# Two graph layers on one core: the destination index read in 2 KB rows and turned on TensorE, and the first three groups of scatters sent to two tables

## The reference

```
layer 1   neigh[src[e]] += edge_weight[e] * x[dst[e]]          for every edge e
          x1 = layernorm(x + branch(x, W_self) + branch(neigh, W_neigh))
          branch(v, W) = standardise(relu(v @ W.T + b)) * scale + offset
layer 2   f = linear(x1); weight = silu(edge_attr_64 @ W_fc1) @ W_fc2
          m[dst[e]] += products of weight, f[src[e]] and edge_attr_4[e]
          out = layernorm(x1 + cos(angle) * sc(x1) + sin(angle) * lin(m))
```

## Time and profile before

| what | value |
|---|---|
| time, median of 3 runs | 5498.28 us (5498.08 to 5500.08) |
| the profiled execution's own time | 5497.89 us |
| its span, first to last instruction | 5496.1 us |
| mean granted TensorE clock | 0.716 of full speed |
| setup, to SP's first load of the node pass | 112.8 us |
| node pass, to the last scatter | about 2956 us |
| all that follows | about 2427 us |

### The profile page before, as it was taken

One profiled execution on the slowest core, in us unless ns is written; L12 is line 12 of the kernel. 1 busy time (PEld: TensorE's weight loads), 2 busy tenths in 40 slices (PEclk: granted clock), 3 DMA queues, 4 the chain that ended last, 5 costly groups with the idle time before them and its releaser, 6 DMA issues. The chain is left out here.

```text
span 5496.1 us, 83091 instructions
## 1 busy us (share of the span) xinstructions
PE 3528.2 (64%) x18413; PEld 2923.1 (53%) x18413; DVE 2741.1 (50%) x11175; ACT 2615.7 (48%) x9201; POOL 4067.5 (74%) x3277
## 2 busy tenths in 40 slices
PE   1555555555555555555555377888888888888872
PEld 0443343344334334334434255888888888888871
DVE  2655555555565555565555384333333333333338
ACT  0322222222222222222222255888888888888863
POOL 0888888888888888888888654777777777777750
PEclk9766666666666666676677577777777777777765
DMA  8666666666666666666665683333333333333323
GB/s 225 120 117 111 111 116 114 112 112 112 111 117 115 111 111 115 116 111 112 112 113 99 130 204 105 81 81 79 81 81 79 81 81 81 79 81 81 79 74 127
DMA packets 748229, 588.07 MB, mean 107 GB/s; under 512 B 336911, under 2 KB 616360, under 8 KB 745111
## 3 DMA queue, kind: packets, MB, share of 16 engines
q0 software_dynamic: 286576, 224.93, 29.6%
q1 hardware_dynamic: 446066, 310.47, 20.9%
q10 hardware_dynamic: 15542, 52.19, 2.4%
HBM read 374.65 MB, written 212.60 MB: 107 GB/s over the span
## 5 line engine op out<-in xcount | busy, mean ns | idle before, releaser
L705 POOL DMA_INDIRECT sums_scratch<-vals,to_i x1568 | 2447.4, 1561 | 616.5 <-issue 506.4
L992 POOL DMA_INDIRECT fg<-f_scratch,src_e x1568 | 1486.4, 948 | 501.6 <-issue 477.3
L1045 ACT ACTIVATE hot<-raw,e_s 128x40 f32<-128x40 f32 x6272 | 1392.3, 313 | 346.2 <-DVE raw L1068 317.5
L619 PE MATMUL ps_n<-same,hot 128*40 128x128 f32 x3136 | 694.3, 414 | 1326.8 <-issue 1324.9
L619 PEld LDWEIGHTS ps_n<-same,hot 128*40 128x40 f32 x3136 | 556.0, 184 | 1436.2 <-issue 1371.8
L662 ACT COPY near<-ps_n 40x512 f32<-40x512 f32 x196 | 113.3, 578 | 1636.3 <-PE ps_n L619 1636.3
L1021 PE MATMUL ps_eu<-hot,prod 128*128 128x120 f32 x3136 | 889.3, 378 | 0.0
L1019 PEld LDWEIGHTS ps_eu<-hot,prod 128*128 128x128 f32 x3136 | 622.3, 244 | 305.4 <-DVE prod L1075 253.9
L1074 DVE TENSOR_TENSOR prod<-ps_ew,fg 128x256 f32<-128x256 f32 x392 | 164.6, 420 | 1239.3 <-DMA fg<-f_scratch,src_e 1239.3
L1019 PE MATMUL ps_eu<-hot,prod 128*128 128x40 f32 x3136 | 618.9, 288 | 248.0 <-DVE prod L1075 247.0
L1021 PEld LDWEIGHTS ps_eu<-hot,prod 128*128 128x128 f32 x3136 | 619.6, 245 | 0.0
(11 more groups left out here) (193 smaller groups left out, 3833.8 us busy)
## 6 DMA issues: line engine op xcount, KB each, us to landing
srow_s<-in_src SPq DMA_DIRECT2D x196, 512.0 KB, 3.5
e_s<-in_edge_attr SPq DMA_DIRECT2D x196, 256.0 KB, 3.7
hid_scratch<-hid SPq DMA_DIRECT2D x196, 256.0 KB, 3.6
hid_e<-hid_scratch SPq DMA_DIRECT2D x196, 256.0 KB
sums_scratch<-zeros ACTq DMA_DIRECT2D x24, 1056.0 KB, 26.8
sums_scratch<-vals,to_i POOLq DMA_INDIRECT x1568
fg<-f_scratch,src_e POOLq DMA_INDIRECT x1568
t_in<-sums_scratch POOLq DMA_DIRECT2D x72, 256.0 KB, 6.7
```

The source lines that it names most:

```text
L619: last = pe.matmul(ps_n[t // TH][:, t % TH, :], hot[:, k, t, :], same[:, k, t, :], start=True, stop=True)
L705: pool.indirect_dma_start(out=sums_d[i], out_offset=bass.IndirectOffsetOnAxis(ap=to_i[:, j, t:t + 1], axis=0), in_=vals[:, j, t, :], in_of ...
L992: pool.indirect_dma_start(out=fg[:, j, t, :], out_offset=None, in_=f_d, in_offset=bass.IndirectOffsetOnAxis(ap=src_s[:, j, t:t + 1], axis= ...
L1045: last = act.activation(hot[:, k, t, c, :], raw[:, k, t, :], ACT.Copy, scale=e4_s[:, j, t, c:c + 1])
```

## The change

Three things change. First, `dst` is loaded in rows of 512 edges (2 KB), one row for a half: 98 partitions by 4 rows, in three transfers. The last row of the last group is filled with FAR beforehand, so only its 320 own edges are loaded. DVE casts it to `dst_r`, takes least and greatest of each half by reducing along the row, and PE turns `dst_r` into the old layout by 16 transposes of strided columns, which DVE copies from PSUM to `dstf`. The chain that computed the extremes over partitions goes. PE does this ahead of the transposes of the weights, and DVE copies `bias4` later. Second, ACT clears the tables in the order of tables, with a semaphore for each. Third, POOL sends the scatters of the first PAIRS = 3 groups to tables 0 and 1 in turn (t % 2), waits for the clearing of tables 0 and 1 before the first scatters of group 0 and for that of tables 2 and 3 at group 3, and its count of earlier scatters to a table follows from that.

```diff
+            dst_i = tmp("dst_i", [98, 4, HE], I32)
+            dst_r = tmp("dst_r", [98, 4, HE])
+            own = tmp("own", [98, HE])
...
-                    full = a["dst"][0:NFULL * SG].rearrange("(s h p k) -> p (s h) k", h=2, p=P, k=TH)
-                    sp.dma_start(dst_i[:, 0:2 * NFULL, :], full).then_inc(dst_in, 16)
-                    sp.dma_start(dst_i[:, 2 * NFULL:NH, :],
-                                 a["dst"][LAST:E].rearrange("(h p k) -> p h k", h=2, p=P)).then_inc(dst2_in, 16)
+                    sp.dma_start(dst_i[:, 0:3, :], a["dst"][0:3 * 98 * HE].rearrange("(g r e) -> r g e", g=3, r=98)).then_inc(dst_in, 16)
+                    sp.wait_ge(far_set, 1)
+                    sp.dma_start(dst_i[0:96, 3, :], a["dst"][3 * 98 * HE:NFULL * SG].rearrange("(r e) -> r e", r=96)).then_inc(dst2_in, 16)
+                    sp.dma_start(dst_i[97:98, 3, TWICE - HE:HE],
+                                 a["dst"][NFULL * SG:E].rearrange("(o e) -> o e", o=1)).then_inc(dst2_in, 16)
...
-                    for z in range(ZSPLIT):
-                        for i in range(NTAB):
+                    for i in range(NTAB):
+                        for z in range(ZSPLIT):
                             act.dma_start(sums_d[i].rearrange("(p r) d -> p (r d)", p=P)[:, z * ZPART:(z + 1) * ZPART],
-                                          zeros[:, :]).then_inc(z_st, 16)
+                                          zeros[:, :]).then_inc(z_st[i], 16)
...
+                    dve.memset(dst_i[:, 3, :], int(FAR)).then_inc(far_set, 1)
                     dve.memset(lin_f[:, :, :], 0.0).then_inc(zeroed, 1)
-                    dve.wait_ge(dst2_in, 16)
                     dve.wait_ge(dst_in, 16)
-                    link(dve.tensor_copy(dstf[:, :, :], dst_i[:, :, :]))
...
+                    dve.tensor_copy(dst_r[:, 0:3, :], dst_i[:, 0:3, :]).then_inc(rows_f, 1)
+                    dve.wait_ge(dst2_in, 32)
+                    dve.tensor_copy(dst_r[:, 3, :], dst_i[:, 3, :]).then_inc(rows_f, 1)
+                    dve.wait_ge(rows_f, 2)
+                    dve.tensor_reduce(ext[:, 0, :], dst_r[:, :, :], AX.X, ALU.min)
+                    dve.tensor_reduce(ext[:, 1, 0:3], dst_r[:, 0:3, :], AX.X, ALU.max)
+                    link(dve.scalar_tensor_tensor(out=own[:, :], in0=dst_r[:, 3, :], scalar=FAR, in1=dst_r[:, 3, :],
+                                                  op0=ALU.is_lt, op1=ALU.mult))
+                    link(dve.tensor_reduce(ext[:, 1, 3:4], own[:, :], AX.X, ALU.max))
...
+                    dve.wait_ge(rows_t, 1)
+                    for k in range(TH):
+                        last = dve.tensor_copy(dstf[:, :, k], ps_d[k][:, :, :].rearrange("p g r -> p (g r)"))
+                    link(last)
+                    dve.tensor_copy(dst0[:, :, :], dstf[:, :, :])
...
+                    pe.wait_ge(rows_f, 2)
+                    for k in range(TH):
+                        for g in range(4):
+                            last = pe.transpose(ps_d[k][:, g, :], dst_r[:, g, k:HE:TH], ident[0:98, 0:98])
+                    last.then_inc(rows_t, 1)
...
-                        pool.wait_ge(z_st, 16 * NTAB * ZSPLIT)
+                        def adds_so_far(i, s, t):
+                            if isinstance(s, int) and s < PAIRS:
+                                return s * 2 * PER + t // 2
+                            return (PAIRS * 2 * PER if i < 2 else 0) + (s - PAIRS) * PER + t // NTAB
...
+                            pair = isinstance(s, int) and s < PAIRS
                             for t in range(TS):
-                                i = t % NTAB
-                                if not isinstance(s, int) or s * PER + t // NTAB > 0:
-
-                                    pool.wait_ge(added[i], s * (16 * PER) + 16 * (t // NTAB))
+                                i = t % 2 if pair else t % NTAB
+                                if isinstance(s, int) and s in (0, PAIRS) and t < NTAB:
+                                    pool.wait_ge(z_st[i], 16 * ZSPLIT)
+                                n = adds_so_far(i, s, t)
+                                if not isinstance(n, int) or n > 0:
+                                    pool.wait_ge(added[i], n * 16)
```

More of the change, by code:

```diff
@@ L48 @@
 ZSPLIT = 6
+PAIRS = 3
 NPAD = 99 * P
@@ L114, in graph_layers @@
         xs_d = nc.dram_tensor("xs_scratch", (NPADB, 2 * D), F32, kind="Internal").ap()
-        passed, cleared, z_st = sem("passed"), sem("cleared"), sem("sums_zeroed")
+        passed, cleared, z_st = sem("passed"), sem("cleared"), [sem(f"sums_zeroed{i}") for i in range(NTAB)]
         sums_d = [nc.dram_tensor(f"sums_scratch{i}", (NPAD, D), F32, kind="Internal").ap() for i in range(NTAB)]
@@ L186, in graph_layers @@
             NCH = NH // 98
-            assert NH == 98 * 4
+            assert NH == 98 * 4 and 2 * NFULL == 3 * 98 + 96 and HE <= TWICE < SG
             with nc.Block() as block:
@@ L283, in _ @@
                     dve.tensor_scalar(spare[:, :], part_f[:, :], float(N), None, ALU.add)
[L284 to L289, removed]
-                    dve.tensor_tensor(diag[:, :, :], ident[0:98, None, 0:98].to_broadcast([98, 4, 98]),
-                                      ext[:, 0, :, None].to_broadcast([98, 4, 98]), ALU.mult).then_inc(diag_d, 1)
-                    link(dve.tensor_reduce(span1[:, :], span[:, :], AX.X, ALU.max))
-                    dve.wait_ge(wts_in, 16 * 8)
-                    dve.tensor_copy(bias4[:, :, :, :], brow[:, :, None, :].to_broadcast([1, 2, CB, D])).then_inc(span_d, 1)
                     dve.wait_ge(span_t, 1)
@@ L308, in _ @@
                     dve.wait_ge(wT_d, 1)
+                    dve.tensor_copy(bias4[:, :, :, :], brow[:, :, None, :].to_broadcast([1, 2, CB, D]))
                     dve.tensor_copy(self_wT[:, :], ps_w[:, 0, :])
@@ L336, in _ @@
                     pe.wait_ge(idn, 4)
+                    pe.wait_ge(rows_f, 2)
[3 more added lines that the diff above has]
+                    last.then_inc(rows_t, 1)
+                    pe.wait_ge(diag_d, 1)
+                    pe.matmul(ps_b[:, :], ones[0:98, :], diag[:, :, :], start=True, stop=True).then_inc(bc_d, 1)
+                    pe.wait_ge(span_d, 1)
+                    pe.transpose(ps_s[:, :], span1[:, :], ident[0:98, 0:98]).then_inc(span_t, 1)
                     pe.wait_ge(wts_in, 16 * 8)
@@ L342, in _ @@
                     pe.matmul(ps_v[:, :, :], ones[0:1, :], rows[:, :, :], start=True, stop=True).then_inc(wT_d, 1)
-                    pe.wait_ge(ext_p, 1)
-                    for c in range(4):
-                        pe.transpose(ps_lo[:, c, :], lo_p[:, 98 * c:98 * (c + 1)], ident[:, :])
-                        last = pe.transpose(ps_hi[:, c, :], hi_p[:, 98 * c:98 * (c + 1)], ident[:, :])
-                    last.then_inc(ext_t, 1)
-                    pe.wait_ge(diag_d, 1)
-                    pe.matmul(ps_b[:, :], ones[0:98, :], diag[:, :, :], start=True, stop=True).then_inc(bc_d, 1)
-                    pe.wait_ge(span_d, 1)
-                    pe.transpose(ps_s[:, :], span1[:, :], ident[0:98, 0:98]).then_inc(span_t, 1)
         def rows_of(t, b):
@@ L709, in _ @@
                         for i in range(NTAB):
-                            pool.wait_ge(added[i], 16 * PER * NSG)
+                            pool.wait_ge(added[i], 16 * adds_so_far(i, NSG, 0))
                         pool.dma_reset(range(min(x.num for x in added), max(x.num for x in added) + 1))
```

26 lines of the change are left out of this document (9 added, 17 removed).

## The result

| what | before | after |
|---|---|---|
| median of the timed runs | 5498.18 us (6 runs) | 5476.8 us (5474.58 to 5479.12, 6 runs) |
| ratio, 95% interval | | 0.9963 [0.9951, 0.9975] |
| span of the profiled execution | 5496.1 us | 5472.8 us |
| first scatter | 142.35 us | 105.90 us |
| first to last scatter | 2924.75 us | 2937.52 us |

The kernel is 21.4 us faster. The span is 23.3 us shorter, and this splits without a rest: the first scatter comes 36.45 us earlier, the scatters take 12.8 us longer, the tail 0.4 us. The tail is less steady than these two profiles make it look: a second profile of the same kernel has 2426.2 us behind its last scatter.

The account below looks back on a forecast made before the run. POOL's scatters bound the node pass, so time before the first scatter counts in full; -35.2 (loads earlier), -1.9 (`hot` ready), +9 (two tables) make -28 us, 5470 us; range 5448 to 5484, the forecast's own 5460 to 5478.

Parts of the forecast that it names:

- The load of `dst` and the chain: Setup: row loads bring `dst_i` at about 5 us, DVE's chain ends at about 24; costed at nothing, ACT still issuing.
- ACT holds the barrier: End of setup: the block ends with ACT's 24th clear issued, at 57.0 us instead of 58.8, bounds 56 and 58.8.
- barrier does not hold ACT: Rival at the setup's end: block ends with DVE at about 24 us, first scatter about 86, 5451 us; chance 0.08.
- SP's first load: Start of the node pass: 2.33 us after ACT's end, at 59.3 us, 53.4 us off 112.77.
- The loads meet the clears: Group 0's loads: pieces alternate with clearing pieces, so `edge_attr_64` is in at 83.4 us, 35.2 us earlier than before.
- group 0 slips through: Rival at group 0's loads: several SP pieces per clear, in at 67 us, 5456 us; chance 0.15, half contention included.
- From there to the first scatter: From `edge_attr_64` landed to POOL's first scatter: 23.7 us less 1.9 since `hot` is ready, so first scatter at 105.2.
- The clears by table: Waits for cleared tables before scatters: tables 0 and 1 clear at about 51 us, others about 86; buys no time.
- Two tables for 24 scatters: POOL's first three groups: pairs caught by SP's loads lose 2.0 us each, 9 us in all, bounds 0 and 24.
- The slower rival: POOL's sequencer at line 702's count: extra operations exposed, 0.35 us per group gives 5537 us; chance of slower 0.04.
- The sum: Whole kernel: -35.2 - 1.9 + 9 = -28 us against the profiled 5497.9 us, giving 5470 us.
- two tables cost more: Rival at the first groups' scatters: up to 24 us instead of 9, 5485 us; chance 0.17, late group 1 loads included.

Follow-up runs that it names:

- the repetition: The changed kernel timed again without further change, on the first chip beside the version with four tables: 5480.95 us, ratio 0.9964 against the kernel before.

## Why the prediction was right, and where it was off

The forecast was 5470 us and the time is 5476.8, inside the forecast's own range, near its upper end; the repetition, at 5480.95, lies outside it and inside the wider range. Most of the steps came as told, one was right by luck (the loads), and one was mis-sized (the two tables). Point by point:

- *The load of `dst` and the chain.* Expected at about 5 us and ended at about 24; 5.7 and 26.0. The four copies from PSUM, for which no row stood, took 2.91 us (taken 2.2, bounds 1 and 4). All of it is hidden, as said.
- *ACT holds the barrier.* 57.0 expected, 56.98 measured. Shown from two sides: with fewer pieces ACT and with it SP come 18 us earlier, with four times as many 20 us later. The rival "barrier does not hold ACT" falls with this.
- *SP's first load.* 59.3 expected, 61.38 measured. Of the 2.1 us, 1.9 are in SP's three register loads behind the barrier (1.08, 0.92 and 0.92 us, where they were 0.45, 0.28 and 0.28). The profile's rows for the second, after and then before (count: ns least/median/most, first and last start):

```profile
L456 SPq TENSOR_LOAD <-near_i x1: 915/915/915, 58.9 to 58.9; - x1
```

```profile
L458 SPq TENSOR_LOAD <-near_i x1: 276/276/276, 111.5 to 111.5; - x1
```

  Today's 2.33 us were measured while little else moved; the new place of the step is beside the clears, and I kept the old price.
- *The loads meet the clears.* 83.4 expected, 85.00 measured; the start was 2.1 us late, so the crawl itself was 0.5 us shorter than forecast. That this is so close is luck, for two steps were off and cancelled. The prediction has the first piece move 1.4 us after its issue, and beside the clears it was 4.3 (65.71 us); its own 22.7 us from there would end at 88.4. And it has group 0 done while clears are left (72 clearing pieces per engine, 66 of group 0). Only 48 were left, the clears ran out at 83.78 us, and the rest of group 0 went unhindered. In each of the eleven profiles in which clears were in the way, group 0's loads are in 1.0 to 3.3 us after the last clearing piece. So the arrival was set by the end of the clears. One for one is shown, at 282/282, 1125/1072 and 432/432, the last with pieces of twice the size. The rival "group 0 slips through" (67 us) falls. The rule of the Trainium skill that the prediction weighed (DMA: Bandwidth & Descriptors, Queues, rings and completion order) would have given 5456 us; between these two queues no run shows it, and the measurement decides.
- *From there to the first scatter.* 21.8 us expected, 20.9 measured; in the experiments this stretch took 20.6 to 23.2 us. First scatter 105.90 against 105.2.
- *The clears by table* buy nothing. On the kernel before, that order with two tables moved the first scatter by 0.9 us only (142.35 to 141.43).
- *Two tables for 24 scatters.* This is the term that was mis-sized: 9 us forecast, 14.0 measured in the first profile (58.87 - 44.87), 15.8 in the second. Of the 23 distances of two scatters between the first and the 25th, 12 are longer than 5 us and average 5.66 us; they form six pairs, in which a scatter lands late, mostly one that shares the engines with loads as in the earlier trace rows, and holds its neighbour up too. 11 are free and average 4.12. The price of a caught pair was right (5.7); but half of the pairs are caught, 6 and not 4.5 (2.7 us more), and a free pair is not free: 0.42 us over 3.7, 2.3 us in sum. The step that failed is "0.3 us to the next issue". POOL starts 0.30 us after its own last instruction, but when it waits for a landed transfer it starts later: a free scatter lands 3.3 us after its start, and the next to its table starts 4.1 us after it, so 0.8 us go by, of which I took 0.3. The row gave the engine's gap, and I used it for a wake-up that no row of before could show, since there four tables hid it. The second profile splits otherwise (ten distances of 6.15 us on average, 13 of 4.30), so the shares are those of one run; the 0.8 us from a landing to the waiting scatter is the same in both.
- *The slower rival.* POOL's sequencer now has three FUSED_REGOPS and one ALU_OP a group in place of two ALU_OPs, and the interval from group 3 on is 1.8656 us against 1.8664: nothing. Its new operations in the kernel after:

```profile
L706 POOLq FUSED_REGOPS  x564: 37/37/71, 174.7 to 2976.8; - x188
...
L706 POOLq ALU_OP  x188: 35/35/45, 180.0 to 2969.6; - x188
```

- *The sum.* -28 forecast, -23.3 in the span: 0.7 us from the first scatter, 3.8 between first and last scatter (14.0 - 9, less 1.2 that the rest of the pass gained), 0.4 in the tail. The other 2.2 us are the profiled execution's lead on the median.

I had "two tables cost more" as a rival of its own and still didn't ask the plainer question, whether this part was worth having. It is a loss in every run: clearing tables 0 and 1 first could only pay if the first scatter came before the last clear, and since group 0's loads end behind the clears, it comes 22 us after it (105.90 against 83.78).

## What to carry to other kernels

Where one queue writes large pieces and another reads small ones, count pieces: each small one waits for a large one, and so one group's loads took 18 us more than alone. If the small queue has more pieces to go than the large one, it ends when the large one ends; then an earlier start wins nothing, and only an earlier end of the large transfers does (12 us of it gave 11 at the first scatter). Look at what holds a barrier: an issue that blocks on a full queue does, and more pieces for the same bytes held it longer. Before a dependence is shortened (here from four tables to two), compare the whole way from issue through landing to the next issue with the new spacing, and take the wake-up from a row where something really waited; and measure each part of a change alone, since here one of three gave back 17 us of 35.

## What the runs showed of the hardware

- How far ACT can issue ahead falls with the pieces in each clear: 12 clears of 16,896-byte pieces were issued by 38.5 us, 24 of 8448 by 57.0, 24 of 2112 only by 77.3, with the same 25.95 MB in all three. Outstanding per engine at the end were 69, 76 and 117 pieces, so it is not a fixed number of pieces.
- Between the hardware queues of SP and ACT the DMA engines took one piece each in turn: 282/282, 1125/1072, 432/432. But SP's first piece moved only 4.2 to 4.5 us after the first issue beside clears, and 1.0 us after it without them. The cause is open.
- Beside full clears most issues of SP take 1.0 to 1.5 us (1.42 for `srow_s`) and not 0.3 to 0.5, and a register load 0.92 us and not 0.28. ACT's clears took 1.26 us each even before its queue was full.
- POOL's issues of plain transfers are never held (24 in 13.3 us), but the end of its block waits for its data; ACT's does not (the barrier opens at about 57 us while its clears move until 83.8).
- After POOL has issued plain clears in the setup, its scatters are 3 to 8 ns longer in the mean of the whole pass (1565 to 1568 ns against 1560 to 1562), in five profiles of three kernels against nine of the others. The cause is open.
- A scatter that waits for a landing starts 0.8 us after it.
